# Routing of part one in slots 22 to 30, its counting in slot 31, and the row maximum behind the second round of top-k

## The chip, the cores and the metric

The kernel runs on one core of a Trainium2 chip. The metric is the device time of one execution in microseconds (us). The engines are called PE (TensorE), DVE (VectorE), ACT (ScalarE), POOL (GpSimd) and SP (SyncE, which issues most transfers).

## What is computed

A small transformer block over 32 images with 32 text tokens each. 36 patches and 32 text tokens make 68 tokens of width 192 per image, 2176 in all.

```python
h = tokens(x, W, b, gamma, beta)                 # five shifted patch sets, einsum, layer norm
h = concatenate([h, txt_weight[x_txt]], axis=1)  # (32, 68, 192)

# attention, 12 heads of 16
qkv = layernorm(h) @ qkv_w.T + qkv_b
true_scores = einsum('bhnd,bhmd->bhnm', q, k) * scale
pred_scores = einsum('bhnd,bhmd->bhnm', ex_quant(q), ex_quant(k))   # powers of two
_, idx = top_k(pred_scores, 32)                  # of 68
attn = scatter(softmax(take_along_axis(true_scores, idx)))
h = h + (attn @ v) @ proj_w.T + proj_b

# feed-forward with two routings, 4 of 128 matrices each
w_fk = topk_sparsify(softmax((x @ W_fk + b_fk) @ emb_fk_n.T), 4)    # x = layernorm(h)
w_rk = topk_sparsify(softmax((x @ W_rk + b_rk) @ emb_rk_n.T), 4)
hh  = einsum('bsnr,bsn->bsr', einsum('bsd,ndr->bsnr', x, f_know), w_fk)
out = einsum('bsnd,bsn->bsd', einsum('bsr,nrd->bsnd', hh, r_know), w_rk)
h = h + out
```

The routing sends each token to only four of the 128 matrices, so the kernel sorts tokens by matrix.

## The kernel before

**Attention.** One image is one batch. A software pipeline of 34 slots, b = 0 to 33, runs on all engines (`slot(b, m)` on each): `slots_of` runs 0 to 32 (L277), and slot 33, `slot(BATCH + 1, 1)`, stands apart. In slot b the front of batch b+1 is made (norm, queries and keys, block-diagonal operands `qbd` and `eqbd` on POOL, scores), top-k of batch b runs on DVE, the back of batch b-1 (mask, maximum, exponential) and the products of batch b-2 (turned probabilities, attention, projection) follow. Scores lie as 7 tiles of 128 x 68.

Top-k of 32 is four rounds of `take8(b, par, r)` (L1422): per round seven MAX8 (L1432) and seven MATCH_REPLACE8 (L1438). The chain of the back is: ACT scales the masked scores (L883) once top-k is over, POOL adds them to the true scores (L704, `masked`), DVE takes the row maximum `smax` (L1503), POOL subtracts it (L715, `shifted`), ACT takes the exponential (L895). POOL's order in a slot is L704, `spread` (L644, `qbd`, waits for the copied queries), L715, `spread_quantised` (L653, `eqbd`, waits for DVE's `ek`, L1419), `rstd` (four small instructions, L677 to L682), `finish(b-3)` (h1 of batch b-3, L636), `residual(b-1)` (L629), then the routing's `t_rstd` and `t_one_hot`. ACT's order puts the score copy (`copy_scores`, L830 and L831) behind the exponential, the output's copy, `scale` (L838, waits for `rstd`) and `t_norm`. DVE starts the next slot when both score copies are there.

**Embedding.** 9 tiles of 128 patches, 24 chunks each (two PE passes a chunk). The first two tiles run ahead; the other 168 chunks are spread over the slots by `EMBED_AT`: 8 a slot to slot 5, then about 7, up to slot 22; the last norm is in slot 23.

**Routing.** h1 is cut into NT = 17 tiles of 128 tokens, in two parts: tiles 0 to 8 (LED = 9) and 9 to 16. `routed(b)` gives the tile of slot b: 24 to 32. In its slot a tile is turned, multiplied to a query and to logits (`t_turn`, `t_query`, `t_logits` on PE), ranked on DVE (`t_rank`: MAX8 L1650, indices, marks) and counted into positions by a one-hot (`t_position`). The slot before does its statistics and its norm (`t_stats`, `t_rstd` on POOL, `t_norm` on ACT, L921). `keep_busy(i)` is ten PE matmuls whose result is not used. Then, ahead of slot 33, part one is counted: `count_part`, `turn_counts`, `sum_counts` on PE in turn with `take_counts`, `form_counts`, `form_base`, `clear_of` on DVE. Part two's tiles follow in `t_step(i)`, which each engine runs for i = 8 to 16 after slot 33; within step i ACT does `t_norm(i + 4)` and DVE ranks tile i + 1.

`find_slots(0, i)` on DVE turns positions into row numbers, in groups of tiles (`FOUND`: 0; 1 and 2; 3 to 5; 6 to 8). `send(i)` on POOL issues four indirect DMAs (L758) that scatter tile i's rows into `slots_x`. POOL runs `t_step(i)` and `send(i - 8)` in turn after slot 33. SP loads part one's rows when all 36 scatters have landed; PE's first product (L1289 turns, L1301 multiplies) needs these rows and `tiles_known`, the end of both parts' routing (L1730). SP loads the last three pieces of `f_all` behind the same semaphore. Part two's scatters and finds run beside part one's products.

## Time and profile before

| | |
|---|---|
| median of 3 runs | 963.44 us (958.73 to 2311.74) |
| the profiled execution's own time | 963.31 us |
| its span | 961.6 us |
| DVE busy | 657.4 us, 68% |
| PE busy | 792.3 us, 82% |
| POOL busy | 565.5 us, 59% |
| ACT busy | 365.6 us, 38% |
| mean granted clock of PE | 0.841 of full speed |

The span lies inside the profiled execution's own time, which has 1.7 us more. Busy time of PE includes waiting in its pipeline. A row of the timeline gives start, duration, engine, line, operation, output and inputs, and in brackets the idle time ahead of it and what ended it. In waits, the engine and line named behind the arrow released the one ahead of it.

### The profile page before, as it was taken

To read this page: it belongs to the slowest core of one execution; us is meant where nothing else is said; L and a number is where in the kernel's file an instruction comes from. 1 tells how busy PE (TensorE), PEld (TensorE's weight loads), DVE (VectorE), ACT (ScalarE), POOL (GpSimd) and SP (SyncE) were. 2 spreads that over 40 slices of the span, in tenths; PEclk is the share of its full clock that TensorE was granted. 3 is DMA by queue.
4 is the path that set the end of the run, shared out by engine and by line. 5 is a ranking of instruction groups with operands and counts; after the bars stand their busy time and mean duration, and the time that the engine had idled before them with its cause. 6 is when DMAs were issued, how large, how long until landed. Compare 5 with 4: busy or idle time off the path is not lost.

```text
span 961.6 us, 22280 instructions
## 1 busy us (share of the span) xinstructions
PE 792.3 (82%) x6347; PEld 658.8 (69%) x6347; DVE 657.4 (68%) x4126; ACT 365.6 (38%) x1147; POOL 565.5 (59%) x788
## 2 busy tenths in 40 slices
PE   5789999999999988898664399999998799499800
PEld 4679888888888767776453277999976558355800
DVE  2298999999999979888577367766763364155433
ACT  0133444444444434544323023444431257345700
POOL 5256666767677656575347507506776577775075
PEclk9787989899999868987655579999996899789955
DMA  9332453535353334531047388756799698489533
GB/s 327 107 121 85 182 181 114 183 113 184 114 183 134 114 116 131 173 113 44 13 134 212 121 254 270 221 156 184 243 403 408 224 327 296 147 299 355 194 100 91
DMA packets 81696, 177.25 MB, mean 184 GB/s; under 512 B 12968, under 2 KB 38344, under 8 KB 78760
## 3 DMA queue, kind: packets, MB, share of 16 engines
q1 hardware_dynamic: 56200, 120.62, 37.7%
q10 hardware_dynamic: 14112, 32.12, 8.9%
q0 software_dynamic: 11264, 23.09, 8.0%
q8 instruction: 54, 0.88, 0.4%
q14 instruction: 66, 0.54, 0.2%
HBM read 94.25 MB, written 81.53 MB: 183 GB/s over the span
## 4 chain that ended last, share of the span: by engine, by line
PE 31%; POOL 27%; DVE 16%; issue 14%; DMA 7%; ACT 4%; SPq 1%; POOLq 0%; ACTq 0%; DVEq 0%
POOL early L781 7%; DVE work L1438 6%; PE bank L1301 5%; POOL slots_g L788 5%; DVE top L1432 4%; PE bank L1289 4%; PE bank L1306 3%; POOL slots_x L758 3%; POOL eqbd L653 3%; PE bank L1103 3%; PE bank L1055 2%; PE bank L1035 2%; PE bank L1353 2%; DMA early<-slots_x 2%; POOL sc L704 2%
## 5 line engine op out<-in xcount | busy, mean ns | idle before, releaser
L1438 DVE MATCH_REPLACE8 work<-top,work 128x68 f32<-128x68 f32 x896 | 179.6, 213 | 0.3 <-issue 0.2
L1432 DVE MAX8 top<-work 128x8 f32<-128x68 f32 x896 | 129.3, 215 | 19.7 <-ACT tru L831 19.2
L1740 DVE COPY place<-bank 96x256 f32<-96x256 f32 x147 | 57.1, 416 | 77.2 <-PE bank L1289 73.8
L781 POOL DMA_INDIRECT early<-slots_h,s_all x68 | 65.8, 967 | 57.0 <-DMA slots_h<-m_y 36.9
L758 POOL DMA_INDIRECT slots_x<-early,s_all x68 | 67.8, 998 | 51.1 <-DVE s_all L1622 30.8
L1035 PE MATMUL bank<-early,xp 128*128 128x192 f32 x432 | 92.8, 378 | 5.6 <-DMA xp<-in_a_x 5.2
L781 POOL DMA_INDIRECT early<-slots_y,s_all x68 | 65.2, 959 | 52.2 <-DMA slots_y<-m_y 29.1
L1035 PEld LDWEIGHTS bank<-early,xp 128*128 128x128 f32 x432 | 89.7, 231 | 8.1 <-DMA xp<-in_a_x 5.5
L1748 DVE COPY place<-bank 128x128 f32<-128x128 f32 x147 | 37.6, 287 | 82.3 <-PE bank L1343 80.3
L704 POOL TENSOR_TENSOR sc<-work,tru 128x476 f32<-128x476 f32 x32 | 38.0, 1188 | 78.5 <-ACT work L883 78.5
L788 POOL DMA_INDIRECT slots_g<-early,s_all x68 | 66.4, 976 | 29.9 <-issue 20.1
L1289 PE MATMUL bank<-ident,early 128*96 128x128 f32 x392 | 69.0, 304 | 14.2 <-DMA early<-slots_x 14.2
L980 ACT ACTIVATE m_y<-bank 128x128 f32<-128x128 f32 x128 | 35.6, 278 | 106.3 <-PE bank L1301 103.9
L644 POOL TENSOR_TENSOR qbd<-qk,head_mask 96x408 f32<-96x408 f32 x64 | 54.3, 868 | 30.9 <-ACT qk L821 30.9
L1438 DVE MATCH_VALUE_LOAD work<-top,work 128x8 f32 x896 | 71.4, 80 | 0.1
L1289 PEld LDWEIGHTS bank<-ident,early 128*96 128x96 f32 x392 | 49.9, 174 | 27.6 <-issue 21.9
L1103 PE MATMUL bank<-v,pT 68*68 68x17 f32 x768 | 61.5, 228 | 6.4 <-ACT pT L853 6.4
L1055 PE MATMUL bank<-xnT,qkv 96*96 96x68 f32 x512 | 56.9, 271 | 10.8 <-ACT xnT L815 10.8
L1103 PEld LDWEIGHTS bank<-v,pT 68*68 68x68 f32 x768 | 59.9, 164 | 7.6 <-ACT pT L853 7.6
L1301 PE MATMUL bank<-f_all,place 96*64 96x128 f32 x768 | 63.0, 305 | 2.4 <-DVE place L1740 2.4
L1003 ACT ACTIVATE m_y<-bank 128x192 f32<-128x192 f32 x128 | 40.4, 331 | 62.5 <-PE bank L1353 61.4
L1055 PEld LDWEIGHTS bank<-xnT,qkv 96*96 96x96 f32 x512 | 52.1, 182 | 15.7 <-ACT xnT L815 15.7
(202 smaller groups left out, 1861.7 us busy)
## 6 DMA issues: line engine op xcount, KB each, us to landing
early<-slots_x SPq DMA_DIRECT2D x49, 384.0 KB, 4.1
slots_y<-m_y ACTq DMA_DIRECT2D x49, 384.0 KB
slots_h<-m_y ACTq DMA_DIRECT2D x49, 256.0 KB
early<-slots_g SPq DMA_DIRECT2D x49, 256.0 KB
f_all<-in_f_know SPq DMA_DIRECT2D x16, 768.0 KB, 8.8
r_all<-in_r_know SPq DMA_DIRECT2D x16, 768.0 KB
slots_x<-zero SPq DMA_DIRECT2D x28, 360.0 KB, 3.0
slots_x<-zero SPq DMA_DIRECT2D x28, 336.0 KB, 3.3
```

What stands on the lines that cost most here:

```text
L704: nc.gpsimd.tensor_tensor(sc1[:, 1 - par], work[:, 1 - par], tru[:, 1 - par], ALU.add).then_inc(sem["masked"], 1)
L758: nc.gpsimd.indirect_dma_start(slots_x[part_of(i)], bass.IndirectOffsetOnAxis(s_all[:, 0, i, k:k + 1], 0), xn_all[:, i, :], None).then_inc ...
L781: nc.gpsimd.indirect_dma_start(g_in[:, i % DEPTH, k, 0:width], None, src, bass.IndirectOffsetOnAxis(s_all[:, r - 1, i, k:k + 1], 0)).then_ ...
L788: nc.gpsimd.indirect_dma_start(slots_g[part_of(i)], bass.IndirectOffsetOnAxis(s_all[:, 1, i, k:k + 1], 0), g_sum[:, i % DEPTH, 0:R], None) ...
L1035: last = nc.tensor.matmul(ps_eo[t % 2], xp[:, t % 2, c, :], wa[:, c, :] if c < 16 else wl[:, c - 16, :], start=(k == 0), stop=(k == CHUNKS ...
L1055: last = nc.tensor.matmul(ps_front[0:HALF, (2 + o) * S:(3 + o) * S], qkv[:, c, o * HALF:(o + 1) * HALF], xnT[:, par, c, :], start=(c == 0) ...
L1103: last = nc.tensor.matmul(ps_o[0:S, head * (HD + 1):(head + 1) * (HD + 1)], pT[:, g, h * S:(h + 1) * S], v[:, par, head, :], start=True, s ...
L1289: last = nc.tensor.transpose(turn_bank[t][0:HALF, c * P:(c + 1) * P], m_x[:, d, t, c:D:2], ident[:])
L1301: last = nc.tensor.matmul(bank[2 + t][rows, 0:R], m_xT[t][0:HALF, c, rows], matrix[:, c * R:(c + 1) * R], start=(c == 0), stop=(c == 1))
L1432: last = nc.vector.max(top8[:, c, :], work[:, par, c, :])
L1438: last = nc.vector.match_replace(work[:, par, c, :], top8[:, c, :], work[:, par, c, :], TAKEN)
L1740: nc.vector.tensor_copy(m_xT[t][0:HALF], turn_bank[t][0:HALF, 0:2 * P].rearrange("p (c s) -> p c s", c=2)).then_inc(sem["m_xt0"], 1)
```

## The change

- Part one is routed two slots earlier, 22 to 30 (`ROUTE0`). SP loads h1 tiles from slot 19, and its waits for stored h1 are at slots 19, 27, 31 and 33.
- The embedding puts 8 chunks into every slot up to 20; the last norm is in slot 21.
- Statistics and norm of the next tile (`ahead_of`) go on through slot 32, so tiles 0 to 11 are normed in slots; only 12 to 16 are left to the steps (`NEXT` = 12).
- Part one's counting, in one piece ahead of slot 33 before, is spread over slot 31 on PE and DVE. Tile 0's slots are found in slot 32, tiles 1 to 3 between slots 32 and 33, 4 to 8 between the steps.
- POOL sends tile 0 and tile 1 ahead of and between the last two `finish`, and tiles 2 to 16 behind them.
- Within a slot: the row maximum stands behind the second round of top-k, not the first; on POOL `spread_quantised` stands ahead of the subtraction; on PE the tile's query stands ahead of attention's products and the logits ahead of `keep_busy`, and the position behind it; on DVE the rank always stands behind round three.

```diff
-ROUTE0 = 24
+ROUTE0 = 22
...
-    EMBED_AT.setdefault(_n // 8 if _n < 48 else 6 + max(_n - 49, 0) // 7, []).append(...)
+    EMBED_AT.setdefault(_n // 8, []).append(...)
...
         def ahead_of(b):
-            return routed(b + 1)
+            return b + 1 - ROUTE0 if ROUTE0 <= b + 1 <= BATCH + 1 else None
+
+        NEXT = BATCH + 2 - ROUTE0
...
@@ SP, slot
-                if b in (20, 30, BATCH + 1):
+                if b in (19, 27, 31, BATCH + 1):
                     all_stored(b - 4)
-                if b == 20:
+                if b == 19:
...
@@ POOL, slot
+                if runs(b, 0, BATCH - 2):
+                    spread_quantised(b + 1)
                 if runs(b, 1, BATCH):
                     pool.wait_ge(sem["smax_done"], b)
...
                     nc.gpsimd.tensor_tensor(sc2[:], sc1[:, 1 - par], smax[:]..., ALU.subtract)
-                if runs(b, 0, BATCH - 2):
-                    spread_quantised(b + 1)
...
-                if b == BATCH + 1:
-                    finish(b - 2, par)
...
             def t_step(i):
-                if follows(i + 4):
+                if i + 4 < NT:
                     t_rstd(i + 4)

             slots_of(pool, slot)
-            for i in range(LED - 4, LED - 1):
-                t_step(i)
-            slot(BATCH + 1, 1)
-            pool.wait_ge(sem["slots_zeroed"], 4 * 16 * N_ZERO)
-            for i in range(LED - 1, NT):
-                t_step(i)
-                send(i - LED + 1)
-            for i in range(NT - LED + 1, NT):
+            pool.wait_ge(sem["slots_zeroed"], 4 * 16 * N_ZERO)
+            send(0)
+            finish(BATCH - 2, 0)
+            send(1)
+            finish(BATCH - 1, 1)
+            for i in range(NEXT - 4, NT):
+                t_step(i)
+                send(i - NEXT + 6)
+            for i in range(NT - NEXT + 6, NT):
                 send(i)
@@ ACT
+                if b == ROUTE0 + LED:
+                    t_placed(LED - 1)
...
-                if follows(i + 4):
+                if NEXT <= i + 4 < NT:
                     t_norm(i + 4)
...
             slots_of(act, slot)
-            t_placed(LED - 1)
-            for i in range(LED - 4, LED - 1):
-                t_step(i)
+            t_step(LED - 2)
             slot(BATCH + 1, 1)
@@ PE, slot
+                i = routed(b)
+                if b == ROUTE0 + LED:
+                    t_position(LED - 1)
                 ... turn_probs, turn_norm, turn_probs
-                i = routed(b)
+                if b == ROUTE0 + LED:
+                    count_part(0)
...
                 if front:
                     queries_keys(b + 1, 1 - par)
+                if i is not None:
+                    t_query(i)
                 if attended:
                     attend(b - 2, par)
-                if i is not None:
-                    t_query(i)
+                if b == ROUTE0 + LED:
+                    turn_counts(0)
                 ... values, embed
                 if i is not None:
-                    if b < BATCH:
-                        keep_busy(i)
+                    t_logits(i)
+                    keep_busy(i)
                     if i >= 1:
                         t_position(i - 1)
-                    t_logits(i)
                 ... turn_out, scores, project_out
+                if b == ROUTE0 + LED:
+                    sum_counts(0)
...
             slots_of(pe, slot)
-            t_position(LED - 1)
-            count_part(0)
-            turn_counts(0)
-            for i in range(LED - 4, LED - 1):
-                t_step(i)
-            sum_counts(0)
+            t_step(LED - 2)
             slot(BATCH + 1, 1)
@@ DVE, slot
+                counting = b == ROUTE0 + LED
+                if b == BATCH:
+                    find_slots(0, 0)
+                i = routed(b)
+                if counting:
+                    take_counts(0)
+                if take:
+                    take8(b, par, 1)
                 if back:
                     dve.wait_ge(sem["masked"], b)
                     nc.vector.tensor_reduce(smax[:], sc1[:, 1 - par], AX.X, ALU.max)
-                i = routed(b)
-                if i is not None and not take:
-                    t_rank(i)
-                if take:
-                    take8(b, par, 1)
...
+                if counting:
+                    form_counts(0)
                 if take:
                     take8(b, par, 2)
-                if i is not None and take:
+                if i is not None:
                     t_rank(i)
+                if counting:
+                    form_base(0)
+                    clear_of(0)
...
             slots_of(dve, slot)
-            for i in range(LED - 4, LED - 1):
-                t_step(i)
-            take_counts(0)
-            form_counts(0)
-            form_base(0)
-            clear_of(0)
+            for i in range(1, 4):
+                find_slots(0, i)
             slot(BATCH + 1, 1)
-            find_slots(0, 0)
             t_step(LED - 1)
-            find_slots(0, 1)
-            find_slots(0, 2)
+            find_slots(0, 4)
+            find_slots(0, 5)
             t_step(LED)
-            for i in range(3, LED):
-                find_slots(0, i)
-                t_step(LED + i - 2)
-            for i in range(2 * LED - 2, NT):
+            find_slots(0, 6)
+            t_step(LED + 1)
+            find_slots(0, 7)
+            find_slots(0, 8)
+            for i in range(LED + 2, NT):
                 t_step(i)
```

## Rows read from the trace of the kernel before

**Rows 1.** Windows: us, PE, PEld, DVE, ACT, POOL busy (instructions), clock, DMA share, GB/s.

```profile
465.00:550.00 85.00, 42.27 (x177) 29.07 (x177) 47.87 (x274) 22.96 (x82) 49.67 (x67) 0.54 0.41 124
```

**Rows 2.** Waits of the whole span: us in total, times, longest.

```profile
DVE top L1432 <- ACT tru L831: 19.2, 10, 5.1
...
DVE top L1650 <- PE bank L1223: 14.1, 10, 3.3
...
DVE smax L1503 <- POOL sc L704: 10.1, 21, 2.0
```

**Rows 3.** Timeline of slot 12 on DVE, POOL and ACT: start us, us, what.

```profile
195.59 1.01 DVE L1432 MAX8 top<-work 128x8 f32<-128x68 f32 x7 [1.69 <-ACT tru L831]
...
200.66 0.98 POOL L715 TENSOR_TENSOR sc<-sc,smax 128x476 f32<-128x476 f32 x1
...
201.22 0.57 DVE L1419 TENSOR_SCALAR ek<-qk 96x272 uint16<-96x272 uint16 x1
...
201.88 1.69 POOL L653 TENSOR_TENSOR eqbd<-ek,head_mask 96x408 bf16<-96x408 bf16 x2 [0.23 <-DVE ek L1419]
...
205.68 0.56 ACT L831 ACTIVATE tru<-bank 128x476 f32<-128x476 f32 x1
...
207.30 1.01 DVE L1432 MAX8 top<-work 128x8 f32<-128x68 f32 x7
```

**Rows 4.** Timeline, first MAX8 of slots 21, 23, 24, 29, 30 and 31.

```profile
302.92 1.01 DVE L1432 MAX8 top<-work 128x8 f32<-128x68 f32 x7
...
326.09 1.01 DVE L1432 MAX8 top<-work 128x8 f32<-128x68 f32 x7 [0.82 <-ACT tru L831]
...
343.86 1.01 DVE L1432 MAX8 top<-work 128x8 f32<-128x68 f32 x7 [4.27 <-ACT tru L831]
...
420.58 1.02 DVE L1432 MAX8 top<-work 128x8 f32<-128x68 f32 x7
...
435.13 1.01 DVE L1432 MAX8 top<-work 128x8 f32<-128x68 f32 x7
...
451.15 1.01 DVE L1432 MAX8 top<-work 128x8 f32<-128x68 f32 x7 [0.24 <-DVE work L1438]
```

**Rows 5.** Windows of two neighbouring routed slots, and slot 11's embedding on PE.

```profile
404.00:420.00 16.00, 14.76 (x96) 12.47 (x97) 14.25 (x108) 6.95 (x23) 9.54 (x16) 0.68 0.57 169
420.00:435.00 15.00, 12.27 (x115) 9.91 (x112) 13.74 (x109) 8.21 (x28) 9.56 (x16) 1.00 0.43 140
...
186.89 4.57 PE L1035 MATMUL bank<-early,xp 128*128 128x192 f32 x14
```

**Rows 6.** Timeline from slot 31's end to tile 0's slots and last sum.

```profile
465.27 0.21 DVE L1438 MATCH_REPLACE8 work<-top,work 128x68 f32<-128x68 f32 x1
...
481.93 0.83 PE L1092 MATMUL bank<-ident,sc 128*68 128x128 f32 x3
...
488.01 0.28 DVE L1591 SCALAR_TENSOR_TENSOR s_at<-place,base 128x128 f32<-128x128 f32 x1
...
490.60 0.16 DVE L1622 CUSTOM_DVE_ANT_0 s_all<-s_i 128x8 uint16<-128x8 uint16 x1
...
490.97 0.58 POOL L636 TENSOR_TENSOR h1b<-pj,hbp 68x192 f32<-68x192 f32 x1 [8.68 <-ACT pj L866]
```

**Rows 7.** Timeline of part one's scatters, routing's end and PE's first product.

```profile
491.51 0.19 POOL L741 TENSOR_TENSOR t_mv<-t_mv,eps_col 128x1 f32<-128x1 f32 x1
...
520.28 0.55 ACT L921 ACTIVATE early<-t_h,t_mv 128x192 f32<-128x192 f32 x1 [5.11 <-POOL t_mv L745]
...
525.52 1.02 POOL L758 DMA_INDIRECT slots_x<-early,s_all  x1 [0.31 <-issue]
...
540.55 0.44 DVE L1730 TENSOR_SCALAR tile_e<-bank 128x272 int32<-128x272 f32 x1 [0.30 <-PE bank L1280]
...
544.56 0.96 POOL L758 DMA_INDIRECT slots_x<-early,s_all  x1 [0.30 <-issue]
...
550.10 1.93 PE L1289 MATMUL bank<-ident,early 128*96 128x128 f32 x8 [9.58 <-DMA early<-slots_x]
```

More of the change, by code:

```diff
@@ L76 @@
 for _n in range((PATCH_TILES - 2) * CHUNKS_K):
-    EMBED_AT.setdefault(_n // 8 if _n < 48 else 6 + max(_n - 49, 0) // 7, []).append((2 + _n // CHUNKS_K, _n % CHUNKS_K))
+    EMBED_AT.setdefault(_n // 8, []).append((2 + _n // CHUNKS_K, _n % CHUNKS_K))
 NORM_AT = {max(b for b, work in EMBED_AT.items() if (t, CHUNKS_K - 1) in work) + 1: t for t in range(2, PATCH_TILES)}
@@ L1683, in t_step @@
             def t_step(i):
-                if follows(i + 4):
+                if NEXT <= i + 4 < NT:
                     t_stats(i + 4)
```

## The prediction

> **What bounds the kernel now.** I read the busy time by stage first. In the slots DVE is the fullest engine, as in one with routing, where it is busy 13.74 of 15 us [rows 5]. The stretch with slots 32 and 33 and part two's routing (465 to 550) has it busy 47.9 of 85, and PE only 42.3 [rows 1]. So that stretch is bound by order, not by work. Behind it lie the two products and the output.
>
> The waits view says what DVE waits for [rows 2]: 19.2 us for the copied scores (L831), 10.1 us in front of the row maximum for POOL's sum (L704, 21 times), 14.1 us in front of the routing's MAX8 (L1650) for PE's logits.
>
> The timeline of slot 12 shows the loop that stands beside DVE's [rows 3]. The slot's first MAX8 starts at 195.59, `ek` ends at 201.79, POOL has the shifted scores (L715) done at 201.64 and then waits for `ek`; `eqbd` ends at 203.57; ACT's score copy, behind POOL's four small normalising steps, starts at 205.68 and ends at 206.24; the next slot begins at 207.30. L715 costs nothing here: its 0.98 us fill POOL's wait for `ek`.
>
> In the routed slots two lengths take turns [rows 4, 5]: 420.58 to 435.13 is 14.55 us at a granted clock of 1.00, and 435.13 to 451.15 is 16.02 us, like its neighbour of 404 to 420, where the clock is 0.68 and PE is busy 14.76 of 16 us. The pair gives 15.28 us a slot. Slot 23 (326.09 to 343.86) takes 17.77, since its last embedding norm and the first `t_norm` stand ahead of the score copy; DVE waits 4.27 us for it.
>
> The stretch from 465 to 550 is the one that the change reshapes [rows 6, 7]. Top-k of slot 31 ends at 465.48. Then come slot 32 with tile 8's rank, the counting, slot 33, and only at 490.76 are tile 0's slots known. POOL works on `t_rstd(12)` from 491.51 and then issues the 36 scatters of part one, the 21st at 525.52, the last at 544.56, thus 1.27 us apart where nothing stands between them. PE's first product starts at 550.10, waiting for the rows' load. The routing's own end, `tile_e`, is there at 540.99, so it has 9.1 us of slack. Everything behind 550.10 starts from that product, and I let it shift as a block.
>
> **The sum.** I make it against the profiled execution (span 961.6, its own time 963.31, beside the median of 963.44; the lowest run shown is 958.73, so one run can be 5 us off).
>
> *Slots 1 to 20 (to the start of slot 21, now 302.92).* Behind the second round, the maximum needs no wait, and `ek` comes at the same place in DVE's order, after rounds one and two and the maximum. So `eqbd` starts no later. But L715 now stands behind `eqbd` on POOL, so the normalising steps, ACT's `xn` and its in-order score copy come 0.98 us later than `eqbd` would let them [rows 3]. Worked for slot 12: `ek` loses some 0.2 of wait ahead of the maximum (an estimate; the mean of the 21 waits is 0.48, the routed slots' among them) and, run after `qbd`, some of its 0.57, and ends about 201.2; `eqbd` 203.0, L715 204.0, the copies 206.6 by the intervals of before. The next slot then starts at 206.9 instead of 207.30. Slots in which DVE is last have under a microsecond of slack for the copy and lose 0 to 0.3. Both together: about 0. The eighth embed chunk adds two passes: in slot 11 14 passes took 4.57 us, thus 0.65 more [rows 5]. It shows only where PE is last, as in slot 11, whose scores made DVE wait 1.69 [rows 3]; I take three such slots at 0.65. Sum +2; bounds -3 (all small waits vanish) and +6 (PE last in nine of 15 slots).
>
> *Slots 21 to 30.* Slot 21 inherits slot 23's collision: 17.3 (17.77 less the small waits). Nine routed slots, 22 to 30, at 15.28 are 137.5. In a clock-bound slot PE's work is the same, since `keep_busy` only moves behind the logits; in a full-clock slot the POOL and ACT loop is as long as before. Against the 148.23 us from 302.92 to 451.15 [rows 4] this is 154.8: +6.6. Two more slots are routed ahead of slot 31, and two less are bare. Bounds: all nine at 14.55 make it -0.0, all at 16.02 make it +13.2.
>
> *Slot 31.* Now 14.33 (451.15 to 465.48). Tile 7's rank goes, the counting comes, both a dozen small DVE instructions; the counting's PE halves lie half a slot ahead of DVE's, and the wait ahead of the maximum goes. I take -0.5, bounds -2 and +1. Call X the end of slot 31's top-k: 465.5 + 2 + 6.6 - 0.5 = 473.6.
>
> *From X to the first product (now 84.6).* In slot 32 `find_slots(0, 0)` takes the 2.75 us it takes now (488.01 to 490.76), over the wait for POOL's sum. POOL ends slot 32 with `t_rstd(11)` at about X + 7.1 and starts the first send there. (An estimate: find's 2.75 from X, a maximum of under a microsecond, L715's 0.98 [rows 3] give X + 4.5, and `finish`, `residual` and `t_rstd` some 2.6 more, as `rstd` and a copy took 2.1 from 203.57.) Four scatters take 5.08 us. `finish(30)`, `send(1)`: X + 18. `finish(31)` waits for slot 33: PE has slot 32's products behind it and runs tile 9's turn and query, to X + 9.2 by my estimate, then turned probabilities, products, normalising, projection and the sum in 9.6 us, as from 481.93 to 491.55 now: h1 at X + 18.7, so this wait costs 0.7 [rows 6]. Behind it the remaining seven tiles: now nine tiles from 491.51 to 545.52 take 54.0, five of them with a `t_rstd`; less two without, 43.9. The last scatter ends at X + 62.6, starts at X + 61.6, and the product follows 5.54 later: X + 67.2 [rows 7]. So -17.4. Bounds: 0.5 us of POOL idle at each of the first three steps, +2; or the sends wait for a late slot 33, +7 (below).
>
> Queued behind the waiting POOL are `t_rstd(12)` and all later sends; behind `t_norm(16)` is the routing's end. `t_norm(16)` started at 520.28 and `tile_e` came 20.7 us later. Now `t_rstd(16)` ends at X + 47.5, so `tile_e` comes at about X + 68.5, or 3 us sooner, since the finds that were mixed into the last steps are over. The slack of 9.1 shrinks to about 0 to 2. SP's three late loads of `f_all` and PE's first product wait for it.
>
> Sum: +2 + 6.6 - 0.5 - 17.4 = -9.3, so the first product at 540.8 and 963.3 - 9.3 = 954. By the Trainium skill (SBUF — State Buffer, Who interferes with whom) a DVE instruction with two SBUF inputs blocks against a GpSimd instruction that reads SBUF, as do copies and scalar forms in a two-port mode, and the later one waits for the whole of the other. L1419, such a scalar form, took 0.57 in slot 12 beside POOL, which fits. By that rule `find_slots(0, 0)` in slot 32, beside POOL's sum, would lengthen X to the first send by up to the length of such a sum, about 1 us, and the sum would be 955.
>
> **The rivals.**
> 1. *Slower: the 0.98 us of L715 is exposed in every slot.* If `ek` doesn't come earlier and DVE stays without slack, ACT's copy is late by 0.98 in each of the 20 slots ahead of slot 21: +19.6 in place of +2, so 972. For it: ACT's copy is what DVE waits for ahead of slots 12, 23 and 24 [rows 3, 4]. Against: in slot 12 the copy ended at 206.24, a microsecond ahead of 207.30 [rows 3]. It decides from 0.55 us a slot, where the gain is gone. 0.13.
> 2. *The routed slots run at one clock.* With the logits ahead of `keep_busy` and no embedding in slots 21 and 22, PE may be granted 2.4 GHz through, nine slots at 14.55: 954 - 6.6 = 947. With 1.2 GHz in most of them, 9 x 0.74 = 6.6 more: 961. For the first: every second slot has it already [rows 5]. 0.13 and 0.09. The skill's TensorE: Matmul & The Clock Gate (What's actually happening) has sustained activity release the default half rate; the rows agree in that the fuller slots are followed by 1.00, but don't say which way two more routed slots push.
> 3. *The change doesn't bring the sends forward.* `finish(31)` stands ahead of 28 of the 36 scatters. If slot 33 ends as late after X as now (491.55 is X + 26.1), the sends lose 7.4: 961. For it: POOL is in order; against: the counting that held slot 33 up is gone from there. 0.12.
> 4. *DVE's waits vanish as a whole*: with the 10.1 and most of the 14.1 us of [rows 2] gone and nothing in their place, another 11: 943. Against: in slots of 16 us PE is last, in those of 14.55 POOL and ACT. 0.06.
> 5. The forecast, 950 to 959: 0.47.
>
> **How the numbers follow.** The range of 944 to 970 runs from rival 4 to just below rival 1 and leaves out about 2 in 10. 2 per cent, about what a measurement of this kernel can tell from no change, is 19.3 us: faster means below 944.1, slower above 982.6. Rival 4, and rival 2's first with luck in slots 1 to 20, give faster 0.07; rival 1 with the low clock gives slower 0.04; the rest is 0.89.
>
> **What would show it.** The first MAX8 of slot 21 near 305; slot 21 17 us, slots 22 to 30 in turn 14.5 and 16; no wait of DVE ahead of the maximum, and L715 behind `eqbd` with ACT's exponential some 2 us later; X near 473.6; the first scatter at X + 7, `finish(31)` near X + 18.7, the last scatter at X + 61.6, `tile_e` within 2 us of the first product, and 411 us behind that product as before. The forecast is wrong if slots 1 to 20 are longer by 0.5 us each, if X is later than 482, if a POOL wait of more than 5 us stands ahead of `send(2)`, or if the stage behind the first product doesn't shift as a block.

## The result and the profile after

| | before | after |
|---|---|---|
| median in the first comparison (4 runs each) | 961.47 us (958.73 to 2311.74) | 944.15 us (943.92 to 945.62) |
| ratio, 95% interval | | 0.9832 (0.9805 to 0.9859) |
| the same kernel again, beside others | 959.39 | 949.31, ratio 0.9871 (0.9835 to 0.9907) |
| and a third time | 962.30 | 950.00, ratio 0.9878 (0.9832 to 0.9925) |
| profiled execution's span | 961.6 | 943.9 |

The change makes the kernel 1.2 to 1.7 per cent faster, 10 to 17 us, which is inside "within 2 per cent". The forecast was 954, which is 7.5 us below the median of 961.47; the first comparison gave 17.3 us, the two later ones 10.1 and 12.3. In the later comparisons the runs of before went from 953.24 to 970.98 us and those of after from 943.57 to 956.49, so four runs of each told less than their interval says. One of the four runs of before took 2311.74 us; the ratios leave such slow runs out, and the means without it are 960.6 and 944.5, 16.1 us apart.

In the profile of after, the stretch that answers to [rows 1] runs from the end of slot 31's top-k to the first product. It is 66.7 us long and no engine is full in it:

```profile
472.90:539.60 66.70, 38.82 (x158) 27.31 (x159) 44.15 (x242) 20.06 (x72) 46.90 (x60) 0.50 0.52 156
```

DVE's waits, as in [rows 2]. The wait ahead of the maximum has no row any more; that for the score copy has grown from 19.2 to 29.2 us, in 17 places for 10:

```profile
DVE top L1435 <- ACT tru L832: 29.2, 17, 5.2
DVE srec L1521 <- PE bank L1104: 12.2, 5, 3.2
DVE top L1661 <- PE bank L1231: 11.8, 5, 4.0
```

Slot 12 on PE, DVE, POOL and ACT, as in [rows 3]. `ek` takes 0.23 instead of 0.57 and ends 5.53 behind the slot's start (6.20 before), `eqbd` (L655) ends 7.30 behind it (7.98 before), and the subtraction (L719) stands behind it. But the copies of the scores now wait for PE, which had 16 embedding passes in front of them. The slot takes 12.91 us (194.73 to 207.64), where [rows 3] have 11.71:

```profile
194.73 1.01 DVE L1435 MAX8 top<-work 128x8 f32<-128x68 f32 x7
...
199.50 4.02 PE L1036 MATMUL bank<-early,xp 128*128 128x192 f32 x16
...
200.03 0.23 DVE L1422 TENSOR_SCALAR ek<-qk 96x272 uint16<-96x272 uint16 x1
...
200.34 1.69 POOL L655 TENSOR_TENSOR eqbd<-ek,head_mask 96x408 bf16<-96x408 bf16 x2 [0.51 <-DVE ek L1422]
202.00 0.98 POOL L719 TENSOR_TENSOR sc<-sc,smax 128x476 f32<-128x476 f32 x1
...
206.36 0.57 ACT L831 ACTIVATE work<-bank 128x476 f32<-128x476 f32 x1 [1.62 <-PE bank L1083]
206.82 0.56 ACT L832 ACTIVATE tru<-bank 128x476 f32<-128x476 f32 x1
...
207.64 0.49 DVE L1435 MAX8 top<-work 128x8 f32<-128x68 f32 x3 [0.54 <-ACT tru L832]
```

The first MAX8 of slots 21, 22, 23, 30 and 31, as in [rows 4]. Slot 21 takes 17.07, with the 4.27 of wait that slot 23 had before:

```profile
304.42 0.23 DVE L1435 MAX8 top<-work 128x8 f32<-128x68 f32 x1 [0.25 <-DVE work L1441]
...
321.49 0.23 DVE L1435 MAX8 top<-work 128x8 f32<-128x68 f32 x1 [4.27 <-ACT tru L832]
...
337.23 0.23 DVE L1435 MAX8 top<-work 128x8 f32<-128x68 f32 x1 [0.22 <-DVE work L1441]
...
441.87 0.23 DVE L1435 MAX8 top<-work 128x8 f32<-128x68 f32 x1 [0.24 <-DVE work L1441]
...
458.77 0.23 DVE L1435 MAX8 top<-work 128x8 f32<-128x68 f32 x1 [1.13 <-ACT tru L832]
```

Windows of slots 28 and 29, as in [rows 5]: two lengths still take turns there, with the two clocks. Slots 22 to 25 don't follow the pattern; by their first MAX8 they take 15.74, 14.46, 14.85 and 13.73:

```profile
411.34:427.78 16.44, 15.35 (x101) 12.94 (x102) 13.38 (x105) 7.39 (x26) 9.52 (x16) 0.69 0.51 154
427.78:441.87 14.09, 11.68 (x110) 9.67 (x109) 13.64 (x104) 7.16 (x25) 9.52 (x16) 0.97 0.45 145
```

Slot 32 on DVE and POOL, as in [rows 6]. X, the end of slot 31's top-k, is at 472.88. The find for tile 0 runs 472.80 to 476.51, the first scatter starts at 481.38, and h1 of the last batch (L638) starts at 492.05 after a wait of 0.17:

```profile
472.67 0.21 DVE L1441 MATCH_REPLACE8 work<-top,work 128x68 f32<-128x68 f32 x1
...
473.69 1.18 POOL L706 TENSOR_TENSOR sc<-work,tru 128x476 f32<-128x476 f32 x1 [5.58 <-ACT work L886]
473.71 1.30 DVE L1614 SCALAR_TENSOR_TENSOR s_hit<-iota_e,idf,s_at 128x128 bf16<-128x128 f32 x1
474.95 0.34 DVE L1614 SCALAR_TENSOR_TENSOR s_hit<-iota_e,idf,s_at 128x128 bf16<-128x128 f32 x1
...
476.35 0.16 DVE L1633 CUSTOM_DVE_ANT_0 s_all<-s_i 128x8 uint16<-128x8 uint16 x1
...
477.27 0.98 POOL L719 TENSOR_TENSOR sc<-sc,smax 128x476 f32<-128x476 f32 x1 [2.40 <-DVE smax L1514]
...
481.38 1.13 POOL L758 DMA_INDIRECT slots_x<-early,s_all  x1 [0.36 <-issue]
...
492.05 0.58 POOL L638 TENSOR_TENSOR h1b<-pj,hbp 68x192 f32<-68x192 f32 x1 [0.17 <-ACT pj L867]
```

The rest up to the first product, as in [rows 7]: the first scatter of tile 2, the last norm, the last scatter of part one, the routing's end, and the product. PE had waited 9.58 us ahead of it before, and waits 1.55 now:

```profile
494.00 1.06 POOL L758 DMA_INDIRECT slots_x<-early,s_all  x1 [0.17 <-issue]
...
519.59 0.55 ACT L924 ACTIVATE early<-t_h,t_mv 128x192 f32<-128x192 f32 x1 [4.22 <-POOL t_mv L745]
...
533.78 1.03 POOL L758 DMA_INDIRECT slots_x<-early,s_all  x1 [0.30 <-issue]
...
538.47 0.44 DVE L1737 TENSOR_SCALAR tile_e<-bank 128x272 int32<-128x272 f32 x1 [0.50 <-PE bank L1283]
...
539.60 0.65 PE L1292 MATMUL bank<-ident,early 128*96 128x128 f32 x2 [1.55 <-DMA early<-slots_x]
```

So the first product is 10.5 us earlier (539.60 for 550.10), and the end is 17.7 earlier. The stretch behind the first product took 411.5 us before and 404.3 after, though no line of it was changed. The expectations below name a mark in it, "the spill": the groups of part one behind the main ones, whose matrices PE picks by numbers read at run time (L1306 before, L1309 after). From the product to the spill it took 60.1 us before and 56.3 after. Where the 7.2 us between 411.5 and 404.3 come from was the first question of the experiments; what the two parts of the slot order and of the embedding are worth was the second.

### The profile page after: what moved, and what is told of

The parts are those of the page before. It is cut to its first block, busy times and chain, and to the rows that moved or that the text cites. A ratio compares the mean times of both kernels' runs of the same rounds, so it can differ in the third digit from the quotient of the medians.

```text
span 943.9 us, 22303 instructions
## 1 busy us (share of the span) xinstructions
PE 789.4 (84%) x6357; PEld 659.8 (70%) x6357; DVE 653.0 (69%) x4126; ACT 362.7 (38%) x1147; POOL 564.5 (60%) x788
## 4 chain that ended last, share of the span: by engine, by line
PE 45%; POOL 25%; issue 11%; ACT 8%; DMA 6%; DVE 4%; SPq 1%; POOLq 0%; ACTq 0%; DVEq 0%
PE bank L1056 6%; POOL early L782 6%; PE bank L1036 5%; PE bank L1356 5%; PE bank L1304 5%; PE bank L1292 4%; PE bank L1358 3%; PE bank L1309 3%; POOL qbd L646 3%; POOL eqbd L655 3%; PE bank L1104 3%; PE bank L1346 3%; PE bank L1081 3%; POOL slots_g L789 3%; POOL slots_x L758 2%
## 5 line engine op out<-in xcount | busy, mean ns | idle before, releaser
L1435 DVE MAX8 top<-work 128x8 f32<-128x68 f32 x896 | 129.7, 215 | 32.6 <-ACT tru L832 29.2
L898 ACT ACTIVATE sc<-sc 128x476 f32<-128x476 f32 x32 | 19.2, 600 | 160.7 <-POOL sc L719 160.7
L1292 PE MATMUL bank<-ident,early 128*96 128x128 f32 x392 | 66.6, 295 | 7.2 <-DMA early<-slots_x 7.2
L655 POOL TENSOR_TENSOR eqbd<-ek,head_mask 96x408 bf16<-96x408 bf16 x64 | 54.1, 865 | 21.0 <-DVE ek L1422 21.0
L1104 PE MATMUL bank<-v,pT 68*68 68x17 f32 x768 | 62.8, 230 | 4.3 <-ACT pT L854 4.3
L1104 PEld LDWEIGHTS bank<-v,pT 68*68 68x68 f32 x768 | 62.1, 167 | 4.8 <-ACT pT L854 4.8
```

The costliest lines, as they stand in the source:

```text
L655: last = nc.gpsimd.tensor_tensor(eqbd[:, g, 0:HH * S].rearrange("p (h s) -> p h s", h=HH), ek[:, g, :].unsqueeze(1).to_broadcast([HALF, HH ...
L1104: last = nc.tensor.matmul(ps_o[0:S, head * (HD + 1):(head + 1) * (HD + 1)], pT[:, g, h * S:(h + 1) * S], v[:, par, head, :], start=True, s ...
L1292: last = nc.tensor.transpose(turn_bank[t][0:HALF, c * P:(c + 1) * P], m_x[:, d, t, c:D:2], ident[:])
L1435: last = nc.vector.max(top8[:, c, :], work[:, par, c, :])
```

## The experiments

For each kernel four stretches were read from its profile: slot 2's first MAX8 to slot 21's (the unrouted slots), slot 21's to slot 31's, X to the first product, and the first product to the end of the span.

| kernel | median us (runs) | slots 2-20 | slots 21-30 | X to product | behind it |
|---|---|---|---|---|---|
| before | 959.4 to 962.3 | 232.5 | 148.2 | 84.6 | 411.5 |
| before, 2nd and 3rd profile | (1 each) | 229.7, 231.5 | 148.2, 146.8 | 84.5, 85.0 | 405.0, 415.2 |
| before, order alone | 956.75 (12) | 226.4 | 148.2 | 85.9 | 415.5 |
| before, eight chunks alone | 971.95 (6) | 239.8 | 151.6 | 84.9 | 409.5 |
| before, order and chunks | 963.54 (12) | 236.3 | 151.4 | 86.3 | 405.0 |
| before, PE kept busy | 961.16 (12) | 231.3, 234.7, 232.6 | 146.6, 146.7, 148.3 | 84.9, 84.9, 84.5 | 403.3, 409.3, 406.8 |
| after | 944.15 (4), 949.31 (6), 950.00 (6) | 233.7, 239.0, 233.7 | 154.4, 155.5, 153.8 | 66.7, 66.6, 66.7 | 404.3, 404.3, 404.6 |
| after, order undone | 959.94 (12) | 236.9, 237.1 | 154.7, 154.8 | 68.2, 67.9 | 416.0, 409.8 |
| the same, PE kept busy | 954.58 (12) | 237.0 | 154.8 | 68.0 | 406.1 |
| after, steps kept busy | 945.26 (6) | 236.0 | 155.4 | 66.5 | 405.1 |
| after, sends later | 950.59 (8) | 230.6 | 157.6 | 70.5 | 404.9 |
| after, rows later | 952.66 (8) | 230.6 | 157.6 | 73.7 | 404.1 |
| after, leaner `t_rstd` | 945.91 (6), 944.39 (6) | 230.7, 233.7 | 153.9, 153.9 | 64.2, 63.9 | 403.3, 405.4 |

One execution's slots 2 to 20 differ from the next one's by up to 8 us in the same kernel (230.6 to 239.0 in the kernels that are alike there), so only means over several profiles are used for them.

### The order inside a slot

First, the kernel after with the order of before:

```diff
@@ DVE, slot
                 if take:
                     take8(b, par, 0)
+                if back:
+                    ... tensor_reduce(smax ...)
...
                 if take:
                     take8(b, par, 1)
-                if back:
-                    ... tensor_reduce(smax ...)
@@ POOL, slot: the subtraction again ahead of spread_quantised(b + 1)
```

> The kernel after, with the order inside a slot as before: the row maximum behind the first round of top-k, and L715's subtraction ahead of eqbd's copy. The theory of the prediction (the new order is worth nothing in slots 1 to 20, and at the first send it costs at most a microsecond): 942 to 946, the same as the kernel after. Rival (the new order is part of the gain, since ek no longer stands behind a wait): 948 to 954, with the wait ahead of the maximum back and the first MAX8 of slot 21 four or more later than its 304.42.

959.94, ratio to before 0.9996 (0.9969 to 1.0022): nothing is left of the gain, and the time lies above both expected ranges. Slot 21's first MAX8 is at 307.78, 3.4 us later. A part of this is the stretch behind the first product (416.0), which is taken up below. The rest is the order's own: slots 2 to 20 average 237.0 in the three profiles with the order undone and 233.5 in eight with it, so about -3.5, with 8 us between the single profiles of the eight; X to the product is 1.3 us longer with it undone, since the maximum then stands ahead of tile 0's find. My theory, that the order is worth nothing, fell.

The converse, the kernel before with these two moves only (the same diff the other way round):

> The kernel before, with only the two moves of the order inside a slot: the maximum behind the second round, eqbd's copy ahead of the subtraction. Theory (nothing in the slots): 958 to 963. Rival (the order is worth some of the gain): 950 to 956. A third reading, the first rival of the prediction, is 964 to 972: the subtraction exposed.

956.75, ratio 0.9974 (0.9949 to 0.9998), between the two ranges. Slots 2 to 20 took 226.4, against 229.7 to 234.7 in six profiles with the order of before. The time of this profile (span 962.6) is longer all the same, for the stretch behind the product took 415.5. In its waits (the view of [rows 2]) the 10.1 us ahead of the maximum are gone. Of them 1.8 come back ahead of the score copy and 3.9 ahead of attention's product (8.8 for 4.9), which leaves 4.4; the logits' wait of the routed slots grows by 6.5, and these slots keep their 148.2.

```profile
DVE top L1432 <- ACT tru L831: 21.0, 14, 5.7
DVE top L1650 <- PE bank L1223: 20.6, 10, 6.0
...
DVE srec L1515 <- PE bank L1103: 8.8, 5, 4.2
```

### Eight chunks in every slot

```diff
-    EMBED_AT.setdefault(_n // 8 if _n < 48 else 6 + max(_n - 49, 0) // 7, []).append(...)
+    EMBED_AT.setdefault(_n // 8, []).append(...)
```

> The kernel before, with only the embedding spread anew: eight chunks in each slot from 6 on in place of seven, so that it ends two slots sooner. The prediction's term: two more passes of 0.33 us in some fifteen slots, seen in three of them, +2, so 961 to 963; slots 20 to 22 may give that back, since they are now bare: 958 to 961. Rival (TensorE is last in most of these slots): +6, 965 to 968.

971.95, ratio 1.0144 (1.0109 to 1.0178), above even the rival's 965 to 968. Slots 2 to 20 took 239.8, and slot 22 and its neighbours gave nothing back: slots 21 to 30 took 151.6, 4.1 more than the 147.5 of the six profiles with seven chunks. Over all profiles with the order of before: 237.0 with eight chunks (three profiles with the routing of after) and 232.1 with seven (six profiles), so +4.9, and 7.7 in this one. Together with the order:

> The kernel before, with the two moves of the order inside a slot and the eight embed chunks a slot, but with the routing and its counting where they were. The order alone gave 956.75 median, the chunks alone 971.95. Theory (both are terms of their own and add: the order takes some 6 us from slots 2 to 21, the chunks add some 6): slot 21 as far behind slot 2 as in the kernel after, 231 to 234 us, time 962 to 968. Rival (with the new order the two extra passes are hidden): slot 21 226 to 228 behind slot 2, time 955 to 959.

963.54, ratio 1.0040 (1.0009 to 1.0072), and slots 2 to 20 took 236.3, 3.4 less than the chunks alone. The median lies in the theory's range, the slots lie above its 231 to 234. About +5 for the chunks and -3.5 for the order is what the slots say over all profiles, and the two seem to be terms of their own. That they simply add isn't shown: the medians were 3.1 us below before for the order, 12.1 above for the chunks, and 4.2 above for both, and these are single profiles.

The kernel after has both. So the rest of the change, the earlier routing and sends, is worth the step from this kernel to the kernel after in the same comparison: 963.54 to 949.31, 14.2 us. Between their profiles the stretch from X to the product is 19.6 us shorter (86.3 to 66.7), and slots 21 to 30 are 4.1 longer (151.4 to 155.5).

### The stretch behind the first product

The windows of before show a granted clock of 0.50 (the lower of the two levels, 1.2 GHz) from the product on for 13 us, those of after for about 3 (columns: window, PE busy with its instructions, granted clock, DMA share, GB/s). Each group of the product that falls into the lower clock takes 2.93 us in place of 1.64. First before, then after:

```profile
550.10:556.10 6.00, 6.00 (x40) 0.50 0.98 286
556.10:562.10 6.00, 6.00 (x46) 0.50 1.02 305
562.10:568.10 6.00, 6.00 (x68) 0.90 0.89 275
```

```profile
539.60:545.60 6.00, 6.00 (x48) 0.69 1.00 283
545.60:551.60 6.00, 5.78 (x75) 1.00 1.03 306
```

My theory was that the 9.58 us in which PE stood idle ahead of the product made the difference. So PE was given matmuls there:

```diff
@@ PE, behind tile_e's product
+            for n in range(21):
+                nc.tensor.matmul(bank[7][:, 0:P], upper_f[:], ident[:], start=True, stop=True)
```

> The kernel before, with 21 f32 matmuls of 128 columns (0.43 us each at 1.2 GHz, 9.0 us in all, into a bank that nobody reads) behind tile_e's product, in the 9.58 us in which TensorE waits for the rows of the first product. The first product can start no sooner than its rows. In four kernels so far the stretch from the first product to the spill's start took 56.3 (after), 60.1 (before), 61.4, 62.8 and 64.0 us, and it followed how long the granted clock stayed at 0.50 in it. Theory (what TensorE did ahead of the first product decides that): the low stretch shrinks from 13 us to at most 4, the stretch to the spill to 56 or 57, the time by 3 to 4 us, so 955 to 957. Rival (the moment at which the clock rises is not set by the work right ahead of it): 59 to 64 us, 957 to 963.

The profiled execution did what the theory wanted, 403.3 behind the product and 54.9 to the spill, with the clock at 1.00 from its first group. The clock rose under the matmuls, so they took 7.3 us and left PE idle for the last 2.4. But this execution, at 954.11, was the fastest of the twelve; their median was 961.16, ratio 1.0017 (0.9985 to 1.0049): no gain. So the idle time was tried from the other side, in the kernel after with its last rows held up (the edit below). The order-undone kernel too was given work there, six such matmuls between `tile_e`'s product and the first product:

```diff
@@ the kernel after, POOL, part one's last tile
                 t_step(i)
+                if i - NEXT + 6 == LED - 1:
+                    for n in range(14):
+                        nc.gpsimd.tensor_tensor(spare[:, n:n + 1], eps_col[:], minus_half[:], ALU.pow)
                 send(i - NEXT + 6)
```

> The kernel after, with fourteen small GpSimd powers (0.57 us each, 8.0 in all, into a scratch of their own) ahead of tile 8's scatters, the last of part one. The routing and tile_e are ready as before; only the rows, and with them the first product, come 8 us later, so TensorE stands idle for some 9.5 us ahead of it, as in the kernel before. Theory: first product at 547 to 549, and then 409 to 416 to the end with 13 to 21 us of low clock: 957 to 964 median. Rival (the rise of the clock doesn't hang on that idle time): 404 behind the first product, 951 to 954.

> The kernel after with the order inside a slot undone (959.94 median; its first product started 5.4 later than after's, and behind it the low clock lasted 18 us in place of 3, so that the end came 17 later), and in addition six f32 matmuls of 128 columns (0.43 us each at 1.2 GHz, into an unread bank) between tile_e's product and the first product, where TensorE waited 2.87 us. Theory (idle TensorE right ahead of the first product costs the clock): behind the first product 404 to 407 in place of 416, median 949 to 953. Rival (the moment of the rise is not set there): median 957 to 961, no change.

With its rows 7.0 us later, PE stood idle for 8.71 us ahead of the product and the clock rose as soon as in after:

```profile
540.83:546.83 6.00, 0.00 (x0) 0.50 0.45 147
546.83:552.83 6.00, 6.00 (x50) 0.70 1.01 289
552.83:558.83 6.00, 5.78 (x75) 1.00 1.04 289
```

404.1 behind the product, median 952.66, where the theory wanted 409 or more and 957 or more. So 8.71 us of idle time ahead of the product don't by themselves bring the long low clock, and 2.87 us of it stood ahead of 19 us of low clock in the order-undone kernel: my theory fell. The kept-busy kernel with the order undone had 406.1 and a median of 954.58, ratio 0.9959 (0.9929 to 0.9989), against 959.94 without it in another comparison. That is 5.4 us faster and between the two expected ranges, in a kernel where the same work in before gave nothing. That the matmuls help there is not excluded; it stays open. The steps ahead of `tile_e` were filled as well:

```diff
@@ the kernel after, PE, t_step(i)
+                if LED - 1 <= i < NT - 4:
+                    for n in range(7):
+                        nc.tensor.matmul(bank[0][:, 0:P], upper_f[:], ident[:], start=True, stop=True)
```

> The kernel after, with seven f32 matmuls of 128 columns into an unread bank at the end of each of the routing's steps 8 to 12 (3.0 us at 1.2 GHz; PE is busy 2.9 of 6.5 us in such a step, and the sends set its length). Theory (clock follows PE's work): the granted clock of 500 to 540 rises from 0.50, tile_e comes 1 to 2 us sooner, the first product is at full clock from its first group: first product at 538.5 to 539.6, 56.3 to the spill becomes 55, the time 940 to 943. Rival (these matmuls get in the way of a step or do nothing to the clock): 943 to 948.

The mean clock from 501 to 540 went from 0.50 to 0.75, and `tile_e` came 64.4 behind X instead of 65.6. The product waited for its rows 2.46 us and stood at X + 66.5 as before. 945.26 lies within the spread of after. PE's faster pace there brought the product no sooner, because its rows come last.

Then the unchanged kernels were profiled again.

> The kernel after, unchanged, run again beside the three kernels below, since the runs of one kernel differ by up to 10 us from one another. Its four runs so far took 943.92 to 945.62; one more profile tells whether the stretch behind the first product (404.3 us to the end, 56.3 to the spill) is this kernel's or that run's. If it is the kernel's: 943 to 948 and 403 to 406 behind the first product. If it is chance: a spread like that of the kernel before, 940 to 955, and up to 412.

> The kernel before, unchanged, for a second profile. If the long low clock at the first product belongs to the kernel: 13 us of it, 60 us to the spill and 410 to 416 to the end. If it belongs to the execution: it may be 3 to 4 us, 56 to the spill and 403 to 406 to the end.

> The kernel before, unchanged, for a third profile; the same two readings: 410 to 416 us behind the first product if it is the kernel's, 403 to 406 in one of the two if it is the execution's.

After had 404.3 again (and 404.6 in its third profile). Before had 405.0 and 415.2. Here are the two, one after the other; ahead of both products PE had stood idle for 9.6 us:

```profile
549.29:555.29 6.00, 6.00 (x52) 0.74 1.03 309
555.29:561.29 6.00, 5.78 (x77) 1.00 1.04 309
```

```profile
548.84:554.84 6.00, 6.00 (x40) 0.50 0.99 289
554.84:560.84 6.00, 6.00 (x46) 0.50 1.02 292
560.84:566.84 6.00, 6.00 (x44) 0.50 0.85 246
```

So the long low clock comes and goes between executions of one kernel. Up to the spill these two took 56.2 and 62.8 us, and the first profile of before 60.1, so the low clock goes with 3.9 to 6.6 us there. The whole stretches differ by more, 6.5 and 10.2 us; the rest lies behind the spill, where no experiment looked. The same holds for before against after: 3.8 of the 7.2 us lie ahead of the spill, and what made the other 3.4 is not shown. Three more profiles asked whether busy matmuls prevent it and whether the order-undone kernel always has it:

> The kernel before with 21 matmuls ahead of the first product, unchanged, second profile. If keeping TensorE busy there prevents the long low clock: 402 to 405 us behind the first product. If not, it may be 409 to 416.

> The same kernel, third profile: 402 to 405 us behind the first product in all three if it prevents the long low clock; 409 to 416 in one of them if it doesn't.

> The kernel after with the order inside a slot undone, unchanged, second profile. If its 416.0 us behind the first product were one execution's: 403 to 406 is as likely. If they are the kernel's: 410 to 416 again. X to the first product 68.2 either way, against 66.7 with the order: the maximum now stands ahead of the find.

409.3, 406.8 and 409.8. The first of them began the product at full clock. PE then waited 2.07 us for a later load of rows, and the clock was down to 0.61 in the window that begins 18 us behind the product's start. In the second the clock fell in the 3.66 us of idle time that the matmuls left ahead of the product, and stayed low for 13 us. So these matmuls don't prevent a low clock; PE busy right up to its rows was not tried. The first, at the product and 18 us later:

```profile
552.12:558.12 6.00, 6.00 (x70) 1.00 1.02 276
...
570.12:576.12 6.00, 5.66 (x47) 0.61 0.91 327
```

What remains is a count. All eight profiles of after and of its variants with the order of after have 403.3 to 405.4, and 56.0 to 57.4 to the spill. Of the twelve others four are like them up to the spill (54.9 to 56.6; 403.3 to 406.1 in all), and eight have 60.1 to 64.1 (406.8 to 416.0 in all). If the twelve without the long stretch were dealt at random over all twenty, all eight of after's kind would be among them about once in 250 times. So the kernel after is likely spared the long low clock, but the groups were drawn after the results and mix several kernels. The three profiles each of before and after, one in three and three in three, don't show it alone. Which part of after would do it was not found: the order undone brings it back (416.0, 409.8), but the order alone in the kernel before doesn't remove it (415.5), and with eight chunks added to that it was gone (405.0, one profile).

### The chain from X to the first product

```diff
@@ the kernel after, POOL, ahead of the first scatter
+            for n in range(7):
+                nc.gpsimd.tensor_tensor(emb_m[:, n:n + 1], eps_col[:], minus_half[:], ALU.pow)
             send(0)
```

> The kernel after, with seven small GpSimd powers of 0.57 us (on a scratch column) ahead of the first scatter, 4.5 to 5 us in all. It computes the same. Theory (the first product starts one for one with the first send): first product 4.5 to 5 later, at 544 to 545, the spill as much later, time 947 to 949. Rival 1 (there is slack from X to the first product): under 2 us. Rival 2 (the moment of the clock's rise hangs on where the first product falls): first product 4.5 to 5 later, but the stretch to the spill 60 to 64 us in place of 56.3, time 950 to 957.

The seven powers took 4.02 us, less than I had worked out, the first scatter moved from X + 8.50 to X + 12.30, and the product from X + 66.7 to X + 70.5: 3.8 us each, one for one. The first product stands on the chain of POOL from the first scatter on. 950.59 is not far from after's median of 949.31, in another comparison; with slots that scatter by 8 us the medians don't resolve 4 us, the intervals between rows do. The moment of the clock's rise did not hang on the later start: 56.2 to the spill.

```profile
482.64 4.02 POOL L768 TENSOR_TENSOR emb_m<-eps_col,minus_half 128x1 f32<-128x1 f32 x7
486.84 1.13 POOL L758 DMA_INDIRECT slots_x<-early,s_all  x1 [0.19 <-issue]
```

The same chain made shorter, for tiles 12 to 16:

```diff
@@ POOL, t_rstd(i)
+                if i >= NEXT:
+                    pool.wait_ge(sem["t_eps"], i + 1)
+                    ... tensor_tensor(mv2[:, 2:3], mv2[:, 1:2], minus_half[:], ALU.pow) -> t_rstd
+                    return
@@ DVE, behind t_aggregate(i + 4)
+                nc.vector.tensor_scalar(mv2[:, 0:1], mv2[:, 0:1], -1.0, None, ALU.mult)
+                nc.vector.tensor_scalar(mv2[:, 1:2], mv2[:, 1:2], EPS, None, ALU.add) -> t_eps
@@ ACT, t_norm(i)
+                nc.scalar.activation(mv[:, 3:4], mv[:, 0:1], ACT.Copy, scale=mv[:, 2:3]) -> t_shift
```

> The kernel after, with two of the three small GpSimd instructions of t_rstd for tiles 12 to 16 moved to DVE (epsilon, and the negative mean) and to ACT (the shift), so that only the power of 0.57 stands between two tiles' scatters. Theory (from X on, POOL's in-order chain of scatters and small steps sets the first product): five times 0.75 us sooner, last scatter of part one 3.7 sooner, tile_e as much sooner, first product near 536 and the time 938 to 941. Rival (another chain, DVE's steps or PE's waits, is as long as POOL's): under 1.5 us sooner, 941 to 944. If the moment of the clock's rise is chance, either can come out up to 8 us longer, with the first product early all the same.

> The kernel after, unchanged, beside the leaner one. Two sets of runs gave 944.2 and 949.3 as medians. 944 to 950, and 403 to 406 behind the first product; one of these executions at 410 or more would say that the kernel after has the long low clock too.

> The leaner kernel (two of three small GpSimd steps of t_rstd for tiles 12 to 16 on DVE and ACT), unchanged from its first run, whose median was 945.91, now beside the kernel after. Theory (POOL's chain from X to the first product counts one for one): 3 to 4 us under the kernel after, with the first product 63.0 to 63.5 us behind X in place of 66.7. Rival (another chain is as long): the same as the kernel after within 1.5 us.

X to the product took 64.2 and 63.9 us in place of 66.7: 2.5 to 2.8 earlier, where 3.7 were expected. The rest is a new wait: the second of the five powers stood 1.33 and 1.10 us for DVE's epsilon (L1669), which now comes ahead of it. The row is from the first of the two profiles:

```profile
497.40 0.57 POOL L740 TENSOR_TENSOR t_mv<-t_mv,minus_half 128x1 f32<-128x1 f32 x1 [1.33 <-DVE t_mv L1669]
```

Between two tiles' scatters only the power is left, as in the second:

```profile
503.75 0.96 POOL L762 DMA_INDIRECT slots_x<-early,s_all  x1 [0.30 <-issue]
504.73 0.57 POOL L740 TENSOR_TENSOR t_mv<-t_mv,minus_half 128x1 f32<-128x1 f32 x1
505.49 1.04 POOL L762 DMA_INDIRECT slots_x<-early,s_all  x1 [0.19 <-issue]
```

Its first median, 945.91, lies above both expected ranges (ratio 0.9848, 0.9814 to 0.9881). In the common comparison it took 944.39 (ratio to before 0.9811, 0.9760 to 0.9862), the kernel after 950.00 (0.9878, 0.9832 to 0.9925). The intervals overlap, so that it beats after is shown by the rows, by 2.5 us or more, and only made likely by the medians. It is likely the fastest version of this study.

## Why the prediction was half right

The terms of the sum, against the means of six profiles with the slots and the tail of before and eight with those of after:

| term | predicted | measured |
|---|---|---|
| slots to 20 (measured from slot 2) | +2 | +1.4 (232.1 to 233.5) |
| slots 21 to 30 | +6.6 | +7.8 (147.5 to 155.3) |
| slot 31 | -0.5 | -0.2 (14.3 to 14.1) |
| X to the first product | -17.4 | -18.0 (84.7 to 66.7) |
| first product | -9.3 | -9.0 |
| behind it | 0 | -6.2 (410.6 in three profiles of before, 404.4 in three of after) |

- **Up to the first product the forecast held**, in the sum within 0.3 us by these means (-10.5 in the two first profiles, -7.4 between three of before and three of after alone, since their slots vary), and in its places: the profiled X at 472.88 for 473.6, the first scatter at X + 8.5 for 7.1, h1 of the last batch started at X + 19.2 for 18.7 with a wait of 0.17 for 0.7, the last scatter at X + 60.9 for 61.6, `tile_e` started 1.1 us ahead of the product and ended 0.7 ahead, the product at 539.60 for 540.8. Rival 3, that `finish(31)` would hold up the sends, is out.
- **The term of slots 1 to 20 was right by cancellation.** I had the order at about 0; it is worth -3.5, since most of the 10.1 us of [rows 2] did go. I had the eighth chunk at 0.65 us in three slots; it costs about 5. That PE's scores come last in more of them than I took is argued from slot 12 after, not counted. Both bounds (-3 and +6) were set for the mixture. Rival 1, the subtraction exposed at 0.98 us in every slot, is wrong: with the order alone the slots were shorter. Rival 4 named the waits as the gain, and their size is a third of what it gave.
- **The later routed slots kept two lengths**, 14.09 and 16.44 to 16.98 where [rows 4, 5] have 14.55 and 16.02, and slots 21 to 30 took 154.4 for the 154.8 of the forecast. Rival 2, one clock for all of them, is out. But slots 22 to 25 were not in turn, and the eight chunks alone had brought these ten slots to 151.6, the order and the chunks to 151.4, with the routing where it was. So a good part of the +7.8 seems to come from the embedding, and not from two more routed slots as the forecast had it: the size was right, the reason only in part.
- **The step that failed** is "Everything behind 550.10 starts from that product, and I let it shift as a block." The prediction put this term at 0 and named it among its signs of being wrong. The block itself took 411.5 us in the profile of before, and 405.0 and 415.2 in its other two, against 404.3, 404.3 and 404.6 in after: 6.2 us less in the mean. I had read a length from one execution as the kernel's. It contained 13 us of low clock where the profile of after has 3, which goes with 3.8 of its 7.2 us; why the rest shortened, and whether the change causes any of it, stays open. My range, 944 to 970, held the time at its lower edge by 0.15 us, which was luck, and the chances left no room for a change in the block. The 9.0 us and the 6.2 us together make 15.2 (13.6 between the spans of three profiles each), below the 17.3 of the first comparison and above the 10.1 and 12.3 of the later ones. The forecast gain of 9.3 is close to these two.
- The base was the smaller fault: the profiled execution's 963.31 lay 1.8 us above the median it was judged by.
- **The find beside POOL was longer.** Tile 0's find took 3.71 us (472.80 to 476.51) where it took 2.75 before. One of its four L1614 instructions, started 0.02 us behind POOL's sum, took 1.30 us in place of 0.34, and ended 0.14 behind it; the other two profiles of after have 1.31 at the same place. By the Trainium skill (SBUF — State Buffer, Who interferes with whom) the later of two such instructions waits for the whole of the other; this trace agrees, and it is the one place of the sum where the rule's 1 us beside the row's 0 was nearer: 0.96.

## What to carry to other kernels

Take the length of an untouched stretch from several executions before you let it shift as a block: here it differed by 10 us in one kernel, so the 7.2 us between two profiles could not be read as an effect of the change. A term that is the sum of two edits should be costed as two, with their bounds apart: the slot order and the embedding moved the slots by about 3.5 and 5 us and the sum by 1.4. Where a chain of in-order scatters sets the next stage, each microsecond put ahead of it or taken out between them counts, and small arithmetic on that queue belongs elsewhere.

## What the runs showed of the hardware

- The granted clock at a stage's start is not set by the kernel alone. With the same instructions in the same order, and PE idle for 9.6 us ahead of the product in each case, it rose about 3, 13 and 19 us behind the product's start in three executions. 21 matmuls in that idle time brought the clock to 1.00 at the product's first group in two of three profiles. In one of these it fell to 0.50 some 19 us later, behind a wait of PE of 2.07 us for rows; in the third it fell in the 3.66 us of idle time that was left.
- The lower clock from the product on for 13 or 19 us in place of 3 goes with 3.9 and 6.6 us up to the spill in three profiles of one kernel (60.1 and 62.8 for 56.2). A group that took 1.64 us at full clock took 2.93 at half.
- Small POOL powers (128x1) that stand back to back take 4.02 us for seven, 0.57 each; the three instructions of `t_rstd` cost 1.40 us from the first one's start to the next scatter (492.60 to 494.00), the power alone 0.76 (504.73 to 505.49).
- A DVE SCALAR_TENSOR_TENSOR of 128x128 that started 0.02 us behind a POOL TENSOR_TENSOR of 1.18 us took 1.30 us in place of 0.34.
